# Four-layer cross-attention kernel: the joint last stage with its context in four groups of 32 rows, and the narrow layer's scores made twice instead of its probabilities being turned

## Chip, cores and metric

One core of one Trainium2 chip. The metric is the device time of one execution in microseconds (us), median over the runs. Everything is fp32.

## What is computed

`x` is [32 batches, 128 tokens, 128], the context is [32, 128, 96]. Four layers follow each other; all have 16 heads:

```python
x = L0(x, ctx)   # self-attention + cross-attention, heads 64 wide, then a gated feed-forward
x = L1(x, ctx)   # cross-attention, heads 8 wide, layer norm, feed-forward, residual
# L2, wide (heads 64 wide):
h = layernorm(x, gamma, beta)
Q, K, V = h @ Wq, ctx @ Wk, ctx @ Wv              # 128 -> 1024, 96 -> 1024, 96 -> 1024
x = x + (softmax(Q K^T) * 64**-0.5) V @ Wo + bo
# L3, narrow (heads 8 wide), no layer norm:
q, k, v = x @ Wq^T, ctx @ Wk^T, ctx @ Wv^T        # 128 -> 128, 96 -> 128, 96 -> 128
x = x + softmax(q k^T * 8**-0.5) v @ Wo^T + bo
```

## The kernel before, in words

Every stage is a block of five hand-written instruction streams (PE, ACT, DVE, POOL, SP) that meet through semaphores. `wide_attention` does L0's two attentions, `feed_forward` L0's feed-forward, `text_attention` L1's attention, `feed_forward` L1's, and `wide_and_narrow` does L2 and L3 together. That last one is the joint last stage, and almost all of the change lies in it.

The stage is a software pipeline over steps `t`. In each step every batch-level operation is done once, for a batch `t + lag`. `step` in each engine's stream writes out the order; the steps 4 to 27 are a hardware loop of four steps a turn (`steps`), the others are written out. The wide layer runs ahead (queries and keys of batch t+2, scores of t+1, weighing of t-1), the narrow layer behind (h and keys of t-1, scores of t-2, the rest of t-3).

PSUM has eight banks. Four are `scores`: the wide scores of a batch fill all four (two in slot 0, two in slot 1), and later in the step the narrow scores of another batch fill the same four. The other four are the ring: `order` (L1290 on) lists twenty fills a step, each fill takes the next bank, and PE may start one when the fill four places before it has been emptied by ACT or DVE.

What the wide layer does, per batch: `w_queries` and `w_keys` (PE, `project_T`, L1484) make the transposed queries and keys in two halves of 4 matmuls each, with 96 context rows for the keys; POOL copies the context of the batch to `w_cT` first. `w_score` (L1450) is 16 matmuls on two row tiles of 64. DVE takes the maxima of both slots and subtracts them in slot 1; ACT exponentiates slot 0 head by head with its sums (`w_exponentiate_0`, 4 heads twice) and slot 1 in one go. POOL divides (`w_divide`), DVE turns 32x32 squares, and SP sends them to DRAM and back (`away`, `back`) so that they land transposed; `w_weigh` (L1529) multiplies them with the values, `w_project_out` (L1569) is 8 matmuls, `w_finish` adds the residual. `w_values` (L1509) is two matmuls of 512 columns over 96 rows.

What the narrow layer does, per batch: POOL copies the rows of x and the context; `n_queries_keys` makes both in one bank; POOL sets the keys of four heads apart with a mask (`n_set_keys_apart`), so that `n_score` (L1467) makes all 16 heads in 4 matmuls of 512 columns on four row tiles of 32, one per bank. DVE and ACT make the softmax as in the wide layer. `n_transpose_probs` (L1477) turns all 16 heads on PE, 16 transposes in four ring banks, which ACT copies back; `n_weigh` (L1542) weighs them, the inverse sums are turned too (L1550), and `n_weighed` multiplies.

`text_attention` (L1's attention) already works in another way, which the change takes over for L3: scores are made once with queries on the partitions (`scores_for_max`, L1017) only so that DVE can find the maxima (L1195), PE turns the maxima, DVE appends them to the queries' spare rows, and the scores are made a second time, already less their maximum and with the keys on the partitions (`scores_less_max`, L1029). Their exponentials need no transposing before they are weighed (L1061). There the maxima banks and the score banks are three each.

## Time and profile before

| | us |
|---|---|
| runs of the kernel before | 1679.09, 1668.0, 1674.45 |
| median | 1674.45 |
| the profiled execution | 1676.32 |
| its span, first to last instruction | 1674.6 |
| mean granted TensorE clock of it | 0.99 |
| joint last stage, from its first matmuls to the end of the span | 1099.6 to 1674.6 |

The profile is of one execution. Busy time of PE is of overlapping matmuls, so what one group of matmuls costs is read from the start of its first to the start of the group behind it, not from its duration. A fp32 matmul is two records ("x8" is four matmuls), a fp32 transpose is one.

### The profile page before, as it was taken

Reading aid. Unit: us, or ns where it says so; the run is one execution under the profiler, and the core shown is the slowest. Engines: PE = TensorE matmul, PEld = TensorE weight load, DVE = VectorE, ACT = ScalarE, POOL = GpSimd, SP = SyncE. Lnnn points to the kernel's source line nnn. Section 1 sums busy time; section 2 is a strip of 40 time slices with the busy share of each in tenths; the row PEclk is TensorE's granted clock in tenths of the full one; section 3 lists DMA queues with packets and bytes.
Section 4 is the critical chain, followed back from the end, with each engine's and each line's share of the span. In section 5 each row is a group of like instructions: output and inputs, shape, how many; then the busy total and the mean of one; then the engine's idle time right before and its main releaser. Section 6 shows DMA issues by size and latency. Waiting matters only on the chain. (4 is left out here: it accounts for less than half of the span.)

```text
span 1674.6 us, 48052 instructions
## 1 busy us (share of the span) xinstructions
PE 1620.9 (97%) x16480; PEld 1348.4 (81%) x16480; DVE 1252.0 (75%) x2424; ACT 1174.7 (70%) x3648; POOL 704.6 (42%) x1027
## 2 busy tenths in 40 slices
PE   7999999999999999989999998988999999999998
PEld 5788888888888888879978887876888888888876
DVE  4877777777777777757767775656888888888885
ACT  4777777777777777743336665455888888888886
POOL 3444444454444444332224442643343444444441
PEclk9999999999999999999999999998999999999999
DMA  6777777788667776740000000014343444344440
GB/s 185 202 190 189 185 189 191 201 217 218 186 183 199 184 186 182 202 135 1 0 2 3 3 3 2 0 40 138 120 142 119 141 120 139 121 139 121 139 130 9
DMA packets 225246, 211.60 MB, mean 126 GB/s; under 512 B 19475, under 2 KB 222805, under 8 KB 225109
## 3 DMA queue, kind: packets, MB, share of 16 engines
q1 hardware_dynamic: 225108, 209.92, 45.4%
q8 instruction: 67, 1.10, 0.3%
q14 instruction: 71, 0.57, 0.1%
HBM read 109.72 MB, written 100.14 MB: 125 GB/s over the span
## 5 line engine op out<-in xcount | busy, mean ns | idle before, releaser
L907 POOL TENSOR_TENSOR L_probs<-L_probs,L_inv_sum 128x1024 f32<-128x1024 f32 x128 | 242.8, 1897 | 87.2 <-DVE L_inv_sum L803 87.2
L691 ACT ACTIVATE L_probs<-L_scores,L_neg_max 128x128 f32<-128x128 f32 x512 | 182.8, 386 | 135.0 <-DVE L_neg_max L783 135.0
L777 DVE TENSOR_REDUCE L_row_max<-L_scores 128x8 f32<-128x1024 f32 x128 | 156.2, 1220 | 41.8 <-PE L_scores L549 41.8
L2128 POOL TENSOR_TENSOR L2L_w_probs<-L2L_w_probs,L2L_w_inv_sum 128x1024 f32<-128x1024 f32 x64 | 121.4, 1896 | 124.2 <-DVE L2L_w_inv_sum L1931 123.7
L809 DVE STREAM_TRANSPOSE L_squares<-L_probs 128x1024 f32<-128x1024 f32 x125 | 153.0, 1224 | 0.3 <-POOL L_probs L907 0.3
L549 PE MATMUL L_scores<-L_kT,L_qT 64*128 64x128 f32 x2048 | 131.8, 278 | 0.9 <-ACT L_kT L680 0.9
L600 PE MATMUL L_ring<-L_probsT,L_v 128*64 128x128 f32 x2048 | 126.6, 276 | 3.9 <-issue 1.8
L600 PEld LDWEIGHTS L_ring<-L_probsT,L_v 128*64 128x64 f32 x2048 | 110.5, 137 | 23.9 <-issue 19.6
L549 PEld LDWEIGHTS L_scores<-L_kT,L_qT 64*128 64x128 f32 x2048 | 119.4, 188 | 12.5 <-ACT L_oT L680 8.1
L793 DVE TENSOR_REDUCE L_sums<-L_probs 128x8 f32<-128x1024 f32 x64 | 78.1, 1220 | 64.8 <-ACT L_probs L698 64.8
L1195 DVE TENSOR_REDUCE L_maxima<-L_s_banks 128x4 f32<-128x512 f32 x128 | 87.5, 688 | 44.6 <-PE L_s_banks L1017 44.6
L1695 ACT ACTIVATE L2L_w_probs<-L2L_scores,L2L_w_neg_max 128x128 f32<-128x128 f32 x256 | 90.4, 371 | 41.7 <-DVE L2L_w_neg_max L1895 41.7
L691 ACT ACTIVATION_READ_ACCUMULATOR L_probs<-L_scores,L_neg_max 128x1 f32 x512 | 115.8, 226 | 0.0
L680 ACT ACTIVATE L_oT<-L_ring 128x512 f32<-128x512 f32 x128 | 76.5, 599 | 39.7 <-PE L_ring L600 39.6
L1884 DVE TENSOR_REDUCE L2L_w_row_max<-L2L_scores 128x8 f32<-128x1024 f32 x64 | 76.7, 1198 | 28.8 <-PE L2L_scores L1450 28.8
L1706 ACT ACTIVATE L2L_n_probs<-L2L_scores,L2L_n_neg_max 128x128 f32<-128x128 f32 x256 | 90.7, 377 | 4.8 <-DVE L2L_n_neg_max L1901 4.1
L1253 POOL TENSOR_SCALAR L_k_apart<-L_qk,quad_mask 128x128 f32<-128x128 f32 x116 | 50.3, 448 | 93.2 <-ACT L_qk L1153 93.2
L680 ACT ACTIVATE L_kT<-L_ring 128x512 f32<-128x512 f32 x128 | 76.8, 600 | 18.2 <-PE L_ring L557 18.2
L2104 POOL TENSOR_TENSOR L2L_n_x_bias<-L2L_n_rows_h,bias_L 128x128 f32<-128x128 f32 x32 | 14.6, 456 | 177.9 <-DVE x L1980 177.8
L680 ACT ACTIVATE L_qT<-L_ring 128x512 f32<-128x512 f32 x128 | 76.2, 595 | 17.3 <-PE L_ring L557 12.0
L1126 ACT ACTIVATE L_exps<-L_t_banks 128x512 f32<-128x512 f32 x128 | 69.4, 597 | 19.7 <-PE L_t_banks L1029 19.7
L1684 ACT ACTIVATE L2L_n_probsT<-L2L_ring 128x512 f32<-128x512 f32 x128 | 70.4, 611 | 17.9 <-PE L2L_ring L1477 17.9
(236 smaller groups left out, 4578.7 us busy)
## 6 DMA issues: line engine op xcount, KB each, us to landing
L_relay<-L_squares SPq DMA_DIRECT2D x125, 512.0 KB, 3.4
L_probsT<-L_relay SPq DMA_DIRECT2D x500, 128.0 KB, 3.7
L2L_relay<-L2L_w_squares SPq DMA_DIRECT2D x62, 512.0 KB, 3.4
L2L_w_probsT<-L2L_relay SPq DMA_DIRECT2D x248, 128.0 KB, 2.9
out_x<-x SPq DMA_DIRECT2D x32, 64.0 KB, 2.7
L0a_wq<-in_L_xattn_Wq SPq DMA_DIRECT2D x2, 256.0 KB, 2.9
L0a_wk<-in_L_xattn_Wk SPq DMA_DIRECT2D x2, 256.0 KB, 3.2
L0a_wv<-in_L_xattn_Wv SPq DMA_DIRECT2D x1, 512.0 KB, 6.3
```

Source lines behind the costliest of these rows:

```text
L549: last = nc.tensor.matmul(scores[:, s, r, i, :], q[part, i, at.n % 2, :], k[part, i, at.n % 2, :], start=True, stop=True, tile_position=(h ...
L600: last = nc.tensor.matmul(to[WIDE * r:WIDE * (r + 1), TOKENS * i:TOKENS * (i + 1)], v[:, at.n % 2, WIDE * h:WIDE * (h + 1)], probsT[:, at. ...
L680: nc.scalar.activation(to, src, ACT.Copy).then_inc(emptied["act"], 1)
L691: done = nc.scalar.activation(slot_probs(at, 0)[:, n, :], scores[:, 0, r, i, :], ACT.Exp, scale=layer_of(at).scale, bias=neg_max[:, n:n + ...
L777: nc.vector.tensor_reduce(row_max[:, s, :], slot(s), AX.X, ALU.max).then_inc(max_ready[s], 1)
L793: nc.vector.tensor_reduce(sums[:, :, 1, :], slot_probs(at, 1).rearrange("p (r i) k -> p r i k", r=2), AX.X, ALU.add).then_inc(sum_ready, 1)
L809: nc.vector.transpose(squares[:, at.n % 2, :, SLOT_HEADS * s:SLOT_HEADS * (s + 1), :] .rearrange("p j h a -> p h j a"), slot_probs(at, s). ...
L907: nc.gpsimd.tensor_tensor(to, to, inv_sum[:, :, s, :].unsqueeze(3) .to_broadcast([TOKENS, 2, GROUP, TOKENS]), ALU.mult).then_inc(divided, 1)
L1195: nc.vector.tensor_reduce(maxima[:, b % 2, g, :, 0:1].rearrange("p j d -> p (j d)"), s_bank(b, g), AX.X, ALU.max, negate=True).then_inc(ma ...
L1695: done = nc.scalar.activation(w_slot(at, 0)[:, h, :], scores[:, 0, r, i, :], ACT.Exp, scale=W.scale, bias=w_neg_max[:, h:h + 1], accum_out ...
L1706: done = nc.scalar.activation(n_slot(at, 0)[:, h, :], scores[:, 0, r, i, :], ACT.Exp, scale=N.scale, bias=n_neg_max[:, h:h + 1], accum_out ...
L2128: nc.gpsimd.tensor_tensor(to, to, w_inv_sum[:, :, s, :].unsqueeze(3) .to_broadcast([TOKENS, 2, GROUP, TOKENS]), ALU.mult).then_inc(w_divid ...
```

## The change

The stage keeps its place and its results; what changes:

- **Context.** A new class `ContextBlocks` holds the transposed context cut into three blocks of 32 rows, each of them four times: on partitions 0-31, 32-63, 64-95 and 96-127. During `text_attention` SP writes `ctxT` to DRAM once and loads eight batches at a time back into one of two buffers, 12 DMAs each; the chunks for batches 16 to 31 are loaded in the stage, at steps 8 and 16. `w_cT` and `n_cT` with POOL's copies go.
- **Keys and values.** The weights are stored per group g of four: `L2_wk` [128, 3, 2, 128], `L2_wv` [128, 3, 256], loaded by 24 DMAs instead of two. `w_keys` is 24 matmuls of 128 columns (three accumulated per result) and `w_values` 12 of 256 columns, each group on its own row tile of 32 and in its own ring bank. Values are now made at step t for batch t.
- **Scores.** `w_score` is cut in two halves with the keys of the next batch between them.
- **Narrow layer.** As in `text_attention`: `n_score_for_max`, `n_find_maxima`, `n_transpose_maxima`, `n_append_maxima`, `n_score_less_max`, `n_exponentiate`, `n_weigh`, then `n_turn_back`, `n_divide`, `n_transpose_o`, `n_project_out`. The 16 transposes of probabilities, the turned inverses, the row sums and POOL's copy of x go. The maxima use slot 0 and the second scores slot 1, two banks each.
- **Who does what.** POOL normalises x for L2 (was DVE), ACT scales the turned h (was DVE).
- **Written out.** All 40 steps are written out; there is no loop and no special last step. The last wide batch's probabilities are turned by PE at the head of step 32.

```diff
-    order = [("w.PV0", -1, "act"), ("w.PV1", -1, "act"), ("w.q0", 2, "act"), ("w.k0", 2, "act"),
-             ("n.T0", -3, "act"), ("n.T1", -3, "act"), ("w.Wo", -1, "dve"), ("n.T2", -3, "act"), ("n.T3", -3, "act"),
...
+    order = [*((f"w.k{g}", 2, "act") for g in CHUNKS_4), ("n.mT", -3, "dve"), ("w.PV0", -1, "act"),
+             ("w.PV1", -1, "act"), ("n.PV", -4, "act"), ("w.q0", 2, "act"), ("n.D", -4, "dve"), ("w.Wo", -1, "dve"),
+             *((f"w.v{g}", 0, "act") for g in CHUNKS_4), ("n.hT", -1, "act"), ("n.oT", -4, "act"),
+             ("w.q1", 2, "act"), ("n.qk", -1, "act"), ("n.v", -3, "act"), ("n.Wo", -4, "dve"), ("w.hT", 3, "act")]
...
+            def n_score_for_max(b, g, h):
+                part = slice(QUAD * g, QUAD * (g + 1))
+                if h == 0:
+                    if g == 0:
+                        pe.wait_ge(n_parts_ready, b + 1)
+                    if g >= 2:
+                        pe.wait_ge(n_max_ready, 4 * b + g - 1)
+                    elif real(b + 3):
+                        pe.wait_ge(w_exp_ready[0], 2 * (b + 3) + 2)
...
+                last = nc.tensor.matmul(s_bank(g)[:, 2 * (1 - h):2 * (1 - h) + 2, :],
+                                        n_q_part[part, b % 2, h, :], n_k_apart[part, b % 2, 2 * h:2 * h + 2, :],
+                                        start=True, stop=True, tile_position=(QUAD * g, 0))
...
+            def w_keys(b):
+                ctx_blocks.await_loaded(pe, b)
+                to = [start_fill(f"w.k{g}", b) for g in CHUNKS_4]
+                for c in range(2):
+                    for r in range(3):
+                        for g in CHUNKS_4:
+                            part = slice(QUAD * g, QUAD * (g + 1))
+                            last = nc.tensor.matmul(to[g][:, TOKENS * c:TOKENS * (c + 1)], W.wk[part, r, c, :],
+                                                    ctx_blocks.of(b)[part, r, :], start=r == 0, stop=r == 2,
+                                                    tile_position=(QUAD * g, 0))
...
+            for t in range(first, last + 1):
...
+                if real(t - 2):
+                    n_find_maxima(t - 2, 0)
+                    n_find_maxima(t - 2, 1)
+                if real(t + 1):
+                    w_add_up(t + 1)
+                if real(t - 2):
+                    n_find_maxima(t - 2, 2)
+                    n_find_maxima(t - 2, 3)
...
+                if t >= 1 and t % ContextBlocks.CHUNK == 0 and t // ContextBlocks.CHUNK + 1 < ContextBlocks.COUNT:
+                    await_filled(sp, "w.v3", t - 1)
+                    ctx_blocks.load(sp, t // ContextBlocks.CHUNK + 1)
```

How the order moves, on PE, from the head of a step. In the first piece L1450 is the wide scores, L1529 the weighing, L1484 queries and then keys, L1477 the turned narrow probabilities, L1569 the output projection, L1467 the narrow scores, L1550 the turned inverses, L1561 the turned x. This is before:

```order
L1450 MATMUL L2L_scores<-L2L_w_kT,L2L_w_qT 128x128 x16
L1529 MATMUL L2L_ring<-L2L_w_probsT,L2L_w_v 64x128 x16
L1484 MATMUL L2L_ring<-L2L_w_hT,L_wq 128x128 x4
L1484 MATMUL L2L_ring<-L2L_w_cT,L_wk 128x128 x4
L1477 MATMUL L2L_ring<-ident,L2L_n_probs 128x128 x8
L1569 MATMUL L2L_ring<-L_wo,L2L_w_oT 128x128 x8
L1467 MATMUL L2L_scores<-L2L_n_k_apart,L2L_n_qT 128x512 x4
L1477 MATMUL L2L_ring<-ident,L2L_n_probs 128x128 x8
L1550 MATMUL L2L_ring<-ident,L2L_n_inv_wide 128x128
L1484 MATMUL L2L_ring<-L2L_w_hT,L_wq 128x128 x4
L1561 MATMUL L2L_ring<-ident,L2L_n_rows_h 128x128
L1484 MATMUL L2L_ring<-L2L_w_cT,L_wk 128x128 x4
```

And now, PE from the head of a step to the output projection (lines of the changed kernel: L1445 wide scores, L1509 keys, L1567 the turned maxima, L1536 weighing, L1579 narrow weighing, L1497 queries, L1590 the weighed rows turned back, L1556 output projection):

```order
L1445 MATMUL L2L_scores<-L2L_w_kT,L2L_w_qT 128x128 x8
L1509 MATMUL L2L_ring<-ctx_blocks,L_wk 128x128 x24
L1445 MATMUL L2L_scores<-L2L_w_kT,L2L_w_qT 128x128 x8
L1567 MATMUL L2L_ring<-ident,L2L_n_maxima 128x128
L1536 MATMUL L2L_ring<-L2L_w_probsT,L2L_w_v 64x128 x16
L1579 MATMUL L2L_ring<-L2L_n_exps,L2L_n_v 32x128 x16
L1497 MATMUL L2L_ring<-L2L_w_hT,L_wq 128x128 x4
L1590 MATMUL L2L_ring<-ident,L2L_n_weighed 128x128 x2
L1556 MATMUL L2L_ring<-L_wo,L2L_w_oT 128x128 x8
```

The keys moved between the halves of the scores, the transposes of probabilities are gone, and the narrow weighing moved ahead of the first queries. Behind it the two narrow score calls, with the values between them, and the end of the step (the second pair of L1460 and L1476 rows of each call reads like the first and is left out here):

```order
L1460 MATMUL L2L_scores<-L2L_n_k_apart,L2L_n_q_part 128x256 x2
L1476 MATMUL L2L_scores<-L2L_n_q_part,L2L_n_k_apart 128x128 x4
...
L1520 MATMUL L2L_ring<-L_wv,ctx_blocks 128x256 x12
L1460 MATMUL L2L_scores<-L2L_n_k_apart,L2L_n_q_part 128x256 x2
L1476 MATMUL L2L_scores<-L2L_n_q_part,L2L_n_k_apart 128x128 x4
...
L1596 MATMUL L2L_ring<-ident,x 128x128
L1600 MATMUL L2L_ring<-ident,L2L_n_rows_o 128x128
L1497 MATMUL L2L_ring<-L2L_w_hT,L_wq 128x128 x4
L1606 MATMUL L2L_ring<-L2L_n_hT,L_wqT 128x128
L1607 MATMUL L2L_ring<-ctxT,L_wkT 128x128
```

The values, which ended the step, now stand between the two calls. On SP's queue at step 8, in the changed kernel (L2000 stores a batch, L2036 loads context, L1984 and L1993 take squares to DRAM and back):

```order
L2000 DMA out_x<-x 128x128
L2036 DMA ctx_blocks<-ctx_turned 32x1024 x12
L1984 DMA L2L_relay<-L2L_w_squares 512x1x256
L1993 DMA L2L_w_probsT<-L2L_relay 32x4x256 x4
L1984 DMA L2L_relay<-L2L_w_squares 512x1x256
L1993 DMA L2L_w_probsT<-L2L_relay 32x4x256 x4
```

The twelve loads are issued ahead of the step's relays; the other steps have the same rows without them.

## Rows read from the trace of the kernel before

**Rows 1.** Busy time in three stretches of the last stage: start, even steps, end (PE, PEld, DVE, ACT, POOL; then PEclk, DMA share, GB/s).
```profile
1099.58:1183.06 83.48, 71.68 (x630) 57.46 (x630) 54.31 (x98) 52.19 (x174) 30.03 (x44) 0.92 0.33 102
1183.06:1617.76 434.70, 432.09 (x4761) 363.62 (x4762) 375.07 (x645) 380.62 (x1327) 183.71 (x258) 1.00 0.44 131
1617.76:1674.60 56.84, 45.77 (x506) 35.96 (x504) 33.73 (x58) 40.77 (x139) 13.44 (x18) 0.94 0.13 40
```
**Rows 2.** PE's timeline in one even step: start us, us, line, out<-in, records.
```profile
1300.19 2.06 PE L1450 MATMUL L2L_scores<-L2L_w_kT,L2L_w_qT 64*128 64x128 f32 x32
...
1305.07 1.06 PE L1484 MATMUL L2L_ring<-L2L_w_cT,L_wk 96*128 96x128 f32 x8
1305.96 1.04 PE L1477 MATMUL L2L_ring<-ident,L2L_n_probs 128*128 128x128 f32 x8
1306.84 1.95 PE L1569 MATMUL L2L_ring<-L_wo,L2L_w_oT 128*128 128x128 f32 x16
1308.72 1.14 PE L1467 MATMUL L2L_scores<-L2L_n_k_apart,L2L_n_qT 32*128 32x512 f32 x8
1309.79 1.09 PE L1477 MATMUL L2L_ring<-ident,L2L_n_probs 128*128 128x128 f32 x8
...
1311.83 1.06 PE L1484 MATMUL L2L_ring<-L2L_w_cT,L_wk 96*128 96x128 f32 x8
1312.82 1.08 PE L1542 MATMUL L2L_ring<-L2L_n_probsT,L2L_n_v 128*32 128x128 f32 x32
...
1314.60 1.02 PE L1509 MATMUL L2L_ring<-L_wv,L2L_w_cT 96*128 96x512 f32 x2
1315.46 0.39 PE L1575 MATMUL L2L_ring<-L_woT,L2L_n_oT 128*128 128x128 f32 x2
...
1316.86 2.06 PE L1450 MATMUL L2L_scores<-L2L_w_kT,L2L_w_qT 64*128 64x128 f32 x32
```
**Rows 3.** PE's timeline in L1's attention: one call of both scores and what follows.
```profile
922.27 0.48 PE L1017 MATMUL L_s_banks<-L_k_apart,L_q_part 32*128 32x256 f32 x2
922.28 0.49 PE L1029 MATMUL L_t_banks<-L_q_part,L_k_apart 32*128 32x128 f32 x4
922.59 0.38 PE L1017 MATMUL L_s_banks<-L_k_apart,L_q_part 32*128 32x256 f32 x2
...
922.81 0.38 PE L1017 MATMUL L_s_banks<-L_k_apart,L_q_part 32*128 32x256 f32 x2
...
923.38 0.33 PE L1050 MATMUL L_b_bank<-ident,L_maxima 128*128 128x128 f32 x1
923.63 1.08 PE L1061 MATMUL L_a_bank<-L_exps,L_v 128*32 128x128 f32 x32
```
**Rows 4.** The page's costliest groups, whole span: busy us, mean ns, idle before and releaser.
```profile
L2128 POOL TENSOR_TENSOR L2L_w_probs<-L2L_w_probs,L2L_w_inv_sum 128x1024 f32<-128x1024 f32 x64 | 121.4, 1896 | 124.2 <-DVE L2L_w_inv_sum L1931 123.7
L1195 DVE TENSOR_REDUCE L_maxima<-L_s_banks 128x4 f32<-128x512 f32 x128 | 87.5, 688 | 44.6 <-PE L_s_banks L1017 44.6
L1695 ACT ACTIVATE L2L_w_probs<-L2L_scores,L2L_w_neg_max 128x128 f32<-128x128 f32 x256 | 90.4, 371 | 41.7 <-DVE L2L_w_neg_max L1895 41.7
L1884 DVE TENSOR_REDUCE L2L_w_row_max<-L2L_scores 128x8 f32<-128x1024 f32 x64 | 76.7, 1198 | 28.8 <-PE L2L_scores L1450 28.8
L1253 POOL TENSOR_SCALAR L_k_apart<-L_qk,quad_mask 128x128 f32<-128x128 f32 x116 | 50.3, 448 | 93.2 <-ACT L_qk L1153 93.2
L1126 ACT ACTIVATE L_exps<-L_t_banks 128x512 f32<-128x512 f32 x128 | 69.4, 597 | 19.7 <-PE L_t_banks L1029 19.7
```
**Rows 5.** Groups by line, 690 to 960 us and 1180 to 1670 us: two kinds of weight load.
```profile
L1029 PEld LDWEIGHTS L_t_banks<-L_q_part,L_k_apart 32*128 32x128 f32 x624 | 37.9, 186 | 0.0
...
L1484 PEld LDWEIGHTS L2L_ring<-L2L_w_hT,L_wq 128*128 128x128 f32 x416 | 50.4, 191 | 4.5 <-issue 4.5
```
**Rows 6.** SP's timeline at the end of L0's attention, one weight load; and DMA issues, the relay.
```profile
732.84 0.43 SPq L187 DMA_DIRECT2D L_wk<-in_L_xattn_Wk  x1
...
L2L_relay<-L2L_w_squares SPq DMA_DIRECT2D x62, 512.0 KB, 3.4
```

More of the change, by code:

```diff
@@ L1296, in wide_and_narrow @@
     LANDED = 16 * SQUARES
-    ring = Ring(order, range(first, last + 1), BATCHES,
-                {LAST_WIDE: last_wide_order, **tail_orders})
+    ring = Ring(order, range(first, last + 1), BATCHES, {LAST_WIDE + 1: turned_by_pe + order})
     chunks = INNER // 128
@@ L1471, in n_transpose_probs @@
-            def n_transpose_probs(at, n):
-                s, r = divmod(n, 2)
-                if r == 0:
-                    pe.wait_ge(n_exp_ready[s], at.times(2, 2) if s == 0 else at.times(1, 1))
-                to = start_fill(f"n.T{n}", at)
-                for i in range(GROUP):
-                    last = nc.tensor.transpose(to[:, TOKENS * i:TOKENS * (i + 1)],
-                                               n_slot(at, s)[:, GROUP * r + i, :], ident[:, :])
-                filled_by(last, f"n.T{n}")
@@ new lines, in w_values @@
+            def w_values(b):
+                to = [start_fill(f"w.v{g}", b) for g in CHUNKS_4]
+                for r in range(3):
+                    for g in CHUNKS_4:
+                        part = slice(QUAD * g, QUAD * (g + 1))
+                        last = nc.tensor.matmul(to[g][:, 0:INNER // 4], ctx_blocks.of(b)[part, r, :], W.wv[part, r, :],
+                                                start=r == 0, stop=r == 2, tile_position=(QUAD * g, 0))
+                        if r == 2:
+                            filled_by(last, f"w.v{g}")
@@ new lines, in n_turn_back, with n_transpose_h @@
+            def n_turn_back(b):
+                await_emptied(pe, "n.PV", b)
+                to = start_fill("n.D", b)
+                for half in range(2):
+                    last = nc.tensor.transpose(to[:, TOKENS * half:TOKENS * (half + 1)], n_weighed[:, half, :],
+                                               ident[:, :])
+                filled_by(last, "n.D")
+            def n_transpose_h(b):
+                await_emptied(pe, "w.Wo", b)
+                filled_by(nc.tensor.transpose(start_fill("n.hT", b)[:, 0:TOKENS], x[:, b, :], ident[:, :]), "n.hT")
@@ new lines, in _, with __init__, of, write @@
+                if real(t + 1) and t + 1 != LAST_WIDE:
+                    away(t + 1, 0)
+                    back(t + 1, 0)
+            sp.wait_ge(stored, 16 * BATCHES)
+class ContextBlocks:
+    CHUNK = 8
+    COUNT = BATCHES // CHUNK
+    ROWS = 32
+    def __init__(self, tile, dram, written, loaded):
+        self.tile, self.dram, self.written, self.loaded = tile, dram, written, loaded
+    def of(self, b):
+        return self.tile[:, b // self.CHUNK % 2, :, b % self.CHUNK, :]
+    def write(self, sp, ctxT):
+        sp.dma_start(self.dram, ctxT[0:CTX, :, :]).then_inc(self.written, 16)
+        sp.wait_ge(self.written, 16)
+    def load(self, sp, n):
+        src = self.dram.rearrange("(r p) b t -> p r b t", p=self.ROWS)
+        for g in range(4):
+            for r in range(CTX // self.ROWS):
+                sp.dma_start(self.tile[self.ROWS * g:self.ROWS * (g + 1), n % 2, r, :, :],
+                             src[:, r, self.CHUNK * n:self.CHUNK * (n + 1), :]).then_inc(self.loaded[n % 2], 16)
+    def await_loaded(self, engine, b):
+        n = b // self.CHUNK
+        engine.wait_ge(self.loaded[n % 2], 16 * 12 * (n // 2 + 1))
```

1140 lines of the change are left out of this document (466 added, 674 removed).

## The prediction

> **What bounds the kernel now.** I read the page's slices first: PE is busy at nine tenths or more nearly everywhere, at the full clock. Then the windows of the stage that changes. In its even middle, 26 steps take 434.70 us, that is 16.72 us a step, and PE is busy 432.09 of it [rows 1]; the other engines have room (ACT 380.62 / 26 = 14.6 us a step, DVE 14.4, POOL 7.1). The reader should see that there nearly nothing waits: PE's timeline of one step runs from 1300.19 to 1316.86, 16.67 us, with each group starting where the one before ends [rows 2]. So a step is the sum of what PE is given, and an instruction taken off PE is worth its whole slot until another engine becomes the bound. At the stage's start (83.5 us, clock 0.92) and end (56.8 us) it is different: PE is busy 71.68 and 45.77 us, and chains of waits decide [rows 1].
>
> **PE's work in a step, part by part.** Slots are from the start of one group to the start of the next.
>
> Removed: two groups of eight transposes, 1306.84 - 1305.96 = 0.88 us for the first and about 0.93 for the second, and the turned inverses, one transpose, 0.88 / 8 = 0.11 [rows 2]. Together -1.92.
>
> Narrow scores: the one call of 1.07 us (1308.72 to 1309.79 [rows 2]) becomes two calls of the kind that L1's attention has, each 923.38 - 922.27 = 1.11 us [rows 3]. +1.15. The turned maxima cost 923.63 - 923.38 = 0.25 there. Three more transposes (two turned back, one of the divided rows) are 0.33. Together +1.73.
>
> Keys: 0.89 (1305.07 to 1305.96) and 0.99 (1311.83 to 1312.82), 1.88 in all [rows 2]. The trace has no row for 24 matmuls on four row tiles. In L1's call the four tiles together finish one round, 128 columns of two passes on each, every 0.22 us (922.59 to 922.81), and 0.32 for the first round (922.27 to 922.59), behind a change of tiling [rows 3]. 24 matmuls are six such rounds: 0.32 + 5 x 0.22 = 1.42. -0.46. The lower end would be that, the upper end is worked out below. Values: 0.86 twice (1314.60 to 1315.46), 1.72 [rows 2]; now 12 matmuls of 256 columns, three a tile, again six rounds, behind a group of the same tiling: 1.31. -0.41.
>
> Changes of tiling: each costs some 0.1 at the first round (0.32 against 0.22 [rows 3]). The scores are cut in two by the keys, which adds two such changes beyond those counted, and narrow weighing now stands behind wide weighing, which is no dearer. +0.2.
>
> Sum: 16.68 - 1.92 + 1.73 - 0.46 - 0.41 + 0.2 = 15.8 us of PE a step. The queries, wide scores, wide weighing (16 matmuls), output projection and narrow weighing stay.
>
> Here a page's rule speaks against the keys. The rows show a weight load of 32x128 at 186 ns and one of 128x128 at 191 ns [rows 5], so cutting 96 rows in three makes three loads of full length out of one. The Trainium skill, TensorE: Matmul & The Clock Gate, section LDWEIGHTS, says just that: the time goes by the columns, not by the rows. If loads went one behind the other it would undo the gain. But L1's call shows 24 of them (12 matmuls of two) in 1.11 us, 46 ns apiece, so loads of different row tiles overlap; the Trainium skill, TensorEngine Tiling (Array Packing), Key Properties, agrees that tiles load and multiply independently. What no row shows is a round with eight of these loads instead of six. Bound from the row: if six loads were just what fits in 0.22 us, eight take 0.29, and the keys cost 6 x 0.07 = 0.44 us more. I take nothing of it, since L1's narrow weighing runs 32 loads, if narrow ones, in 1.08 us, and keep 0.44 for the range.
>
> **Waits in the new step.** I laid one step out from the durations. Start of wide scores 0; second half done at 3.4 (1.0 + 1.42 + 1.0). DVE: second row maxima and subtraction, 1.2 each [rows 4], then the appended maxima, two 128x128 operations, 0.6 by my estimate from 0.69 for 512 columns [rows 4]: 6.7. The ring bank of the first queries is the one of the turned maxima, so the queries start at 6.8; PE alone would be there at 6.7. Queries full at 7.9; ACT copies (0.5) and does four heads of the wide exponentials (4 x 0.37, overlapping by a tenth: 1.4 [rows 4]): 9.9. The first narrow call waits for them, because it uses the same banks; PE would be there at 9.9 too. That call to 11.0; then the values cover DVE's two maxima (2 x 0.69 [rows 4]) and ACT's two exponentials (2 x 0.60 [rows 4]): second call at 12.4, where PE alone would have started at 12.3. To 13.5, then 0.3 + 0.9 + 0.5 + 0.5, and the last fill of the ring waits for ACT's copy of the second queries until about 15.8. Step 16.0. So I take 0.2 us of waits on top of 15.8. Queued behind the waiting narrow call are values, second queries and the next step's scores, and behind these all of DVE's and ACT's next step; there is no cover for a longer wait.
>
> Room elsewhere: DVE loses two row maxima, the subtraction and the sums of the narrow layer (4 x 1.2) and gets four maxima (2.8) and small ones, so about 13 of 16. ACT loses four copies of a bank and the eight heads with accumulators and gets four exponentials: 11 to 12. POOL gets six operations of 0.45 [rows 4] beside two divisions of 1.9 [rows 4] and the normalising: 8.5. Its longest order, division, then the six, is done at about 7.5, ahead of the narrow call at 9.9. None of the three bounds by its sum.
>
> 26 steps x (16.72 - 16.0) = -18.7 us.
>
> **Start, end, transfers.** Start: the narrow layer's x no longer goes through POOL's queue, and values are a step later. Laid out the same way, the first three steps come to 10 to 14 us less than before; but part of what was lost there is a clock of 0.92 with PE busy 71.68 of 83.48 us [rows 1], which a less busy PE won't better. I take -7, between 0 and -14. End: one wide weighing and projection moves a step later and the two narrow calls have no values between them (1.3 us of waits twice), while the last full steps are shorter: +1, between -5 and +8.
>
> SP: a DMA occupies its queue 0.43 us [rows 6]. The 24 loads instead of two at the end of L0's attention are 22 x 0.47 = 10 us, which there ends beside PE's tail with about as much room; +0.5, between 0 and 3. During L1's attention SP has nothing else. In the stage, 12 context loads (5.6 us of queue, 1.57 MB) stand twice ahead of a relay that is due at about 8 us of the step. It goes off about 4 us late and behind those bytes; it needs 3.4 us out [rows 6], and about 5 us for its four parts to be issued and to land; it has about 5 us of room. +4 for both, between 0 and 12. Written-out code instead of a loop: L1's attention is written out as well and keeps 0.22 us rounds [rows 3]; 0.
>
> Sum: -18.7 - 7 + 1 + 0.5 + 4 = -20.2 us. The profiled execution took 1676.3 (span 1674.6 and 1.7 around it), so 1656.1 on its terms; the median shown is 1.9 below the profiled one, well inside the 11 us that the three runs spread over. I forecast 1656.
>
> **Rivals.**
>
> *PE alone decides* (0.2). The three tight places do not wait and the start gives all of its 14: 26 x 0.2 = 5 and 7 more off: 1644. For it: the step before shows no waits with ACT at 14.6 of 16.7. Against: the banks of the maxima are two here and three in L1.
>
> *Weight loads bind the keys* (0.12). 26 to 31 batches x 0.44 = 11 to 14 more: 1668. For it: 186 ns a load whatever the rows [rows 5]; against: 24 of them in 1.11 us.
>
> *The context loads delay the relay* (0.1). 12 instead of 4: 1664, two steps longer by 6 us each and nothing else.
>
> *Handovers, slower than before* (0.13). The chain wide scores - DVE - queries - ACT - narrow call - DVE - second call - end of step has about eight handovers between engines, and I gave each 0.1 to 0.2 us. My chain is as long as PE's own work, so every bit more lands on the step: it is even with before at 0.09 us more each (0.72 / 8), and at 0.2 more the step is 17.6, 26 x 0.9 = +23: 1676 + 23 - 1.5 = 1698. In L1's attention DVE's maxima already waited 44.6 us in all for scores [rows 4], a sign that the loop of scores and maxima is a loop of latencies; there three banks hid it. Against: most of these places have cover of another group on PE.
>
> *It doesn't do what it says.* If rows of 32 did not run side by side, keys would take 24 x 0.22 = 5.3 us. L1's call excludes it.
>
> The forecast itself has 0.45.
>
> **How the numbers follow.** The forecast's own range is 1648 to 1665. For 8 in 10: the low end takes PE alone, with some of the end, 1638; the high end takes loads binding and a few tenths of handovers, 1676; beyond lie 0.08 above and about as much below. A measurement of this kernel tells about 1% from no change, 16.7 us, so faster means under 1657.7: all of PE alone, and seven tenths of the forecast's weight, some of the small rivals: 0.56. Same, up to 1691: 0.34. Slower: 0.10, the far part of the handovers.
>
> **What would show it.** Right: even steps of 15.9 to 16.2 us in PE's timeline; keys 1.4 us and values 1.3 from their start to the next group; no idle before the second narrow call above 0.2; ACT about 12 us a step. Wrong: rounds of the keys at 0.29 us; PE idle before L1460 on ACT's exponentials or DVE's maxima by more than 0.3; idle before L1536 at steps 9 and 17 of over 3 us; a step over 16.6.

## The result, and the profile after

The changed kernel takes 1689.3 us (median of 6 runs, 1683.2 to 1693.4), the kernel before 1674.4 (6 runs): a ratio of 1.0087, 95% interval 1.0057 to 1.0117. The forecast was 1656, with 1638 to 1676 as the range. What was measured lies 13 us above the range, in what the prediction had as "Same, up to 1691" (chance 0.34). It was wrong, in size and in sign.

The two profiled spans are 1688.1 and 1674.6 us, 13.5 apart. Four stretches hold all of it. The windows of the last stage after, in the columns of [rows 1]:

```profile
core 0: us, PE busy (x) PEld busy (x) DVE busy (x) ACT busy (x) POOL busy (x), PEclk, DMA share, GB/s
1108.66:1182.55 73.89, 63.61 (x894) 56.72 (x894) 47.51 (x83) 47.43 (x160) 36.24 (x52) 0.95 0.38 115
1182.55:1620.75 438.20, 426.13 (x6812) 386.42 (x6811) 310.82 (x566) 315.41 (x1016) 226.38 (x334) 1.00 0.46 138
1620.75:1688.10 67.35, 55.56 (x717) 46.16 (x716) 25.30 (x57) 28.76 (x81) 18.73 (x33) 0.83 0.13 40
```

| stretch | before [rows 1] | after | difference | forecast |
|---|---|---|---|---|
| ahead of the last stage | 1099.58 | 1108.66 | +9.1 | +0.5 |
| its start | 83.48 | 73.89 | -9.6 | -7 |
| 26 even steps | 434.70 | 438.20 | +3.5 | -18.7 |
| its end | 56.84 | 67.35 | +10.5 | +1 |

So there are three causes to find, and one of them lies 350 us ahead of the last stage. (For the context loads, which fall into the even steps, the forecast had +4 besides.) The even step is 16.85 us (438.20 / 26), not 16.0. PE's timeline of one of them:

```profile
start us, us, engine line op out<-in xcount [idle before <-releaser]
1317.27 1.16 PE L1445 MATMUL L2L_scores<-L2L_w_kT,L2L_w_qT 64*128 64x128 f32 x16
1318.37 1.62 PE L1509 MATMUL L2L_ring<-ctx_blocks,L_wk 32*128 32x128 f32 x48
1319.92 1.16 PE L1445 MATMUL L2L_scores<-L2L_w_kT,L2L_w_qT 64*128 64x128 f32 x16
1321.01 0.33 PE L1567 MATMUL L2L_ring<-ident,L2L_n_maxima 128*128 128x128 f32 x1
...
1327.58 0.48 PE L1460 MATMUL L2L_scores<-L2L_n_k_apart,L2L_n_q_part 32*128 32x256 f32 x2 [0.17 <-ACT L2L_w_probs L1681]
...
1329.97 0.57 PE L1460 MATMUL L2L_scores<-L2L_n_k_apart,L2L_n_q_part 32*128 32x256 f32 x2
...
1331.36 0.33 PE L1596 MATMUL L2L_ring<-ident,x 128*128 128x128 f32 x1
...
1333.20 0.39 PE L1617 MATMUL L2L_ring<-L_woT,L2L_n_oT 128*128 128x128 f32 x2
1333.79 0.30 PE L1562 MATMUL L2L_ring<-ident,L2L_w_rows_h 128*128 128x128 f32 x1 [0.20 <-ACT L2L_w_qT L1670]
1334.13 0.38 PE L1445 MATMUL L2L_scores<-L2L_w_kT,L2L_w_qT 64*128 64x128 f32 x2
```

Read as in [rows 2], from one start to the next: keys 1.55 us, the two narrow calls with the values between them 3.78 (1327.58 to 1331.36), and two places where PE waits for ACT. They look small, 0.17 and 0.20, but the second leaves 0.59 between the starts of the two last fills for work of 0.22.

The 26 steps are not all alike. Steps 4 to 28 take 16.83 to 16.88 us and step 29, the last of the stretch, 16.22; but step 17, right behind the second context load, takes 17.89, and there PE stands still between the two halves of the weighing. SP's issues of step 16, then PE in step 17:

```profile
1390.64 5.43 SPq L2036 DMA_DIRECT2D ctx_blocks<-ctx_turned  x12
1396.16 0.52 SPq L1984 DMA_DIRECT2D L2L_relay<-L2L_w_squares  x1
1402.10 1.75 SPq L1993 DMA_DIRECT2D L2L_w_probsT<-L2L_relay  x4
```

```profile
1407.45 1.09 PE L1536 MATMUL L2L_ring<-L2L_w_probsT,L2L_w_v 128*64 128x128 f32 x16 [0.89 <-ACT L2L_w_oT L1670]
```

The profile names ACT's copy, which was done at 1407.29, but by the trace the last of the relay's four parts landed at 1407.36, and PE's next matmul starts 0.09 us later. The way out to DRAM behind the context loads took 5.9 us (1396.16 to 1402.10) where the page's median is 3.2. So the context loads cost about 1.05 us here, and the other steps take 16.83.

Ahead of the stage, the end of L0's attention and the start of L0's feed-forward. SP's issues there first (the last of the 24 pieces), then PE, after:

```profile
743.13 0.57 SPq L188 DMA_DIRECT2D L_wk<-in_L_xattn_Wk  x1
743.74 0.58 SPq L188 DMA_DIRECT2D L_wv<-in_L_xattn_Wv  x1
...
749.77 0.58 SPq L188 DMA_DIRECT2D bias_L<-in_L_xattn_bo  x1
```

```profile
744.56 2.05 PE L644 MATMUL L_ring<-L0b_wo,L_oT 128*128 128x128 f32 x16
750.81 4.60 PE L131 MATMUL L0ff_gate<-ident 128*128 128x128 f32 x20 [4.20 <-PEq L404]
...
758.12 1.06 PE L2136 MATMUL L0ff_gate<-L0ff_hT,wp 128*128 128x256 f32 x2
...
763.24 0.70 PE L2136 MATMUL L0ff_gate<-L0ff_hT,wp 128*128 128x256 f32 x2
```

The same place before:

```profile
743.74 2.05 PE L625 MATMUL L_ring<-L0b_wo,L_oT 128*128 128x128 f32 x16
746.45 2.47 PE L131 MATMUL L0ff_gate<-ident 128*128 128x128 f32 x20 [0.66 <-PEq L385]
...
751.70 0.60 PE L2284 MATMUL L0ff_gate<-L0ff_hT,wp 128*128 128x256 f32 x2
```

An issue takes 0.57 us and not the 0.43 of [rows 6]. SP ends at 750.35, PE's last group at 746.61, and the block ends with the later of them: PE is idle 4.20 us for 0.66. Then its granted clock is at the lower level, 0.50 of full speed from 750.81 to 763.24: the twenty records of `keep_clock` take 4.60 us for 2.47, and until 763.24 the feed-forward's groups stand 0.85 apart for 0.43. The sum: PE 0.82 late already, 3.54 of wait, 2.13, and six groups times 0.42, 2.5: 9.0 of the 9.1 us. Each of these is one execution against one; the medians of experiment 1 put the loads at 6.2 us.

### The profile page after: what moved, and what is told of

It is laid out like the page before. It is cut to its first block and busy times, and to the rows that moved or that the text cites. A ratio compares the mean times of both kernels' runs of the same rounds, so it can differ in the third digit from the quotient of the medians.

```text
span 1688.1 us, 51406 instructions
## 1 busy us (share of the span) xinstructions
PE 1622.8 (96%) x19008; PEld 1386.1 (82%) x19008; DVE 1172.6 (69%) x2330; ACT 1094.0 (65%) x3264; POOL 760.0 (45%) x1126
## 5 line engine op out<-in xcount | busy, mean ns | idle before, releaser
L1841 DVE TENSOR_REDUCE L2L_n_maxima<-L2L_scores 128x4 f32<-128x512 f32 x128 | 82.4, 687 | 32.0 <-PE L2L_scores L1460 32.0
L1691 ACT ACTIVATE L2L_n_exps<-L2L_scores 128x512 f32<-128x512 f32 x128 | 69.7, 602 | 27.4 <-PE L2L_scores L1476 27.4
L1670 ACT ACTIVATE L2L_w_kT<-L2L_ring 128x256 f32<-128x256 f32 x128 | 38.8, 389 | 71.6 <-PE L2L_ring L1509 71.6
L1460 PE MATMUL L2L_scores<-L2L_n_k_apart,L2L_n_q_part 32*128 32x256 f32 x512 | 77.4, 396 | 7.5 <-ACT L2L_w_probs L1681 5.1
```

What stands on the lines that cost most here:

```text
L1460: last = nc.tensor.matmul(s_bank(g)[:, 2 * (1 - h):2 * (1 - h) + 2, :], n_q_part[part, b % 2, h, :], n_k_apart[part, b % 2, 2 * h:2 * h + ...
L1691: nc.scalar.activation(n_exps[:, b % 2, GROUP * g:GROUP * (g + 1), :].rearrange("p h q -> p (h q)"), t_bank(g).rearrange("p j q -> p (j q) ...
```

## Experiments

All ratios are to the kernel before (1674 to 1675 us), with the 95% interval. The heads of the even steps and the windows are read as above. Apart from experiment 4, whose interval reaches past it, all of these kernels lie less than 2% from the kernel before, so differences are small and are told with their intervals. A profile is of one execution, which need not be the median one.

### 1. The loads, somewhere else

The whole list of L2's loads moves from the last step of L0's attention to `first_context_blocks`, which SP runs in L1's attention.

```diff
-            if t == 2 * BATCHES:
-                load_norm(sp, "L2", "L2_ln", "L2_xattn_gamma", "L2_xattn_beta")
...
             ctx_blocks.load(sp, 1)
+            load_norm(sp, "L2", "L2_ln", "L2_xattn_gamma", "L2_xattn_beta")
+            load(sp, "L2", W["L2", "q"][:, :], a["L2_xattn_Wq"])
...
```

> The changed kernel with all loads of the last stage's wide layer issued by SP in L1's attention, behind the first two context blocks, instead of the last step of L0's attention. Theory (SP's 24 issues of 0.58 us end after TensorE's last matmul there, the block's end waits for them, and TensorE's clock is low for some 12 us after): L0ff's first matmuls start about 4.3 us earlier than in the changed kernel, at about 746.5, at the higher clock, L0ff's own turn near 758.6, and the last stage's first matmuls near 1100; time about 1680 (1677 to 1683), which still is above the kernel before, since the last stage alone is 4.4 us longer. Rival (the pieces are hidden, and the 9 us before the last stage come from elsewhere, such as the placement of the tiles): time within 2 us of 1689.

Measured: 1683.1 us, 1.0053 (1.0037 to 1.0068), at the upper end of what was expected. The idle time at the block's end is 0.66 again, and the last stage begins at 1096.93. So the loads' place is the cause of what was lost ahead of the stage. The time fell by 6.2 us and not by 9: in this execution the stage's start took 77.94 us at a clock of 0.91 instead of 73.89 at 0.95. Step 16.85, end 68.3, as after. Whether that start is chance or comes of the move stayed open; in the eight kernels below that are built on this one, the last stage begins anywhere from 1096.2 to 1102.1 and its start takes 73.7 to 78.4 us, so a single profile can't tell a difference of 5 or 6 us there from chance.

### 2. The pieces alone, in the kernel before

```diff
-                load_wide(sp, "L2", "L2", "", CTX)
...
+                for g in range(4):
+                    for r in range(CTX // 32):
+                        for w in ("k", "v"):
+                            load(sp, "L2", W["L2", w][32 * r:32 * (r + 1), 256 * g:256 * (g + 1)],
+                                 a[f"L2_xattn_W{w}"][32 * r:32 * (r + 1), 256 * g:256 * (g + 1)])
...
```

> The kernel before, where alone the last stage's key and value weights are loaded in 24 pieces of 32 rows and 256 columns, with nothing else changed. Theory: SP's issues end some 5 to 10 us later, behind TensorE's end of L0's attention, so time 1674.4 plus 7 to 10, about 1683, all of the loss ahead of the last stage (its start near 1108), the stage itself 575 us. Rival (cost hidden beside TensorE's tail, as the prediction had it): +0.5 us, at most 3.

Measured: 1675.5 us, 1.0008 (0.9991 to 1.0025). No loss that can be measured. The theory as I had put it fell, and the timeline says why. SP, then PE:

```profile
744.42 0.42 SPq L187 DMA_DIRECT2D L_wv<-in_L_xattn_Wv  x1
744.88 0.43 SPq L187 DMA_DIRECT2D L_wo<-in_L_xattn_Wo  x1
745.36 0.58 SPq L187 DMA_DIRECT2D bias_L<-in_L_xattn_bo  x1
```

```profile
746.39 2.47 PE L131 MATMUL L0ff_gate<-ident 128*128 128x128 f32 x20 [1.25 <-PEq L392]
```

As many transfers with as many bytes, but 0.42 us each, not 0.57. SP ends at 745.94, beside PE's tail to within a microsecond, and behind that wait of 1.25 us the granted clock is still 1.00. The number of pieces was not the cost; their form is what differs.

### 3. Which form

```diff
                 for g in range(4):
                     for r in range(CTX // 32):
                         load(sp, "L2", W["L2", "k"][32 * g:32 * (g + 1), r, :, :], keys[g][:, r, :, :])
+                for g in range(4):
+                    for r in range(CTX // 32):
                         load(sp, "L2", W["L2", "v"][32 * g:32 * (g + 1), r, :], values[g][:, r, :])
```

> The changed kernel with its 24 pieces still issued at the end of L0's attention, but all 12 of the keys (three-dimensional: two runs of 128 columns) ahead of all 12 of the values (one run of 256 columns). Theory (an issue of 0.58 us is due to the form of the keys' pieces, and the values' pieces took as long only because they stood behind one): keys 0.57 us, values 0.42 to 0.45 as in before_pieces; SP ends at 748.5 instead of 750.4, TensorE waits about 2.4 us instead of 4.2 at the block's end; if that wait still lowers the clock, time 1687, if it does not, 1683. Rival (both forms take 0.58 here whatever their order): time 1689.

Measured: 1684.4 us, 1.0061 (1.0040 to 1.0082).

```profile
734.60 8.22 SPq L188 DMA_DIRECT2D L_wk<-in_L_xattn_Wk  x12
742.86 5.69 SPq L188 DMA_DIRECT2D L_wv<-in_L_xattn_Wv  x12
```

```profile
750.10 4.04 PE L131 MATMUL L0ff_gate<-ident 128*128 128x128 f32 x20 [2.23 <-PEq L406]
...
756.94 0.59 PE L2143 MATMUL L0ff_value<-L0ff_hT,wp 128*128 128x256 f32 x2
```

From start to start a keys' piece (32 rows of two runs of 128 columns) takes 0.69 us and a values' piece (32 rows of one run of 256) 0.47, that is 0.43 and the gap. The two together are 0.58 in the mean: in the changed kernel the dear and the cheap ones shared it. The Trainium skill, DMA: Bandwidth & Descriptors, section "Why a DMA increments its semaphore by 16 and not by 1", says that "One descriptor moves one contiguous run of the last dim", so a keys' piece needs twice as many; and the Trainium skill, Perfetto Trace Analysis, DMA Instruction — HWDGE, counts the wait for the descriptor generator into the time shown for an issue, which would be why a values' piece looks dear behind a keys' piece. That these are the mechanism no run here shows. Behind PE's wait of 2.23 us the clock was still low, but only until the feed-forward's groups (0.59 us at 756.94, where 0.59 is the higher level). SP ended only 0.7 us earlier than after (749.64) and PE's last group 1.3 later. The profiled spans are 2.4 us apart, all of it ahead of the last stage (1106.32); the medians are 4.9 apart. The theory had the cause right and the keys' price too low (0.57 expected), so SP ended 1.1 us later than it said.

### 4. Without the row tiles

The keys and values in their old form, from `ctxT`; the narrow layer and the written-out code as changed. The context blocks and their loads are gone, ScalarE copies two banks of 512 columns where it copied four of 256, and the values, the ring's order and the weights' loads change to match (not shown).

```diff
             def w_keys(b):
-                ctx_blocks.await_loaded(pe, b)
-                to = [start_fill(f"w.k{g}", b) for g in CHUNKS_4]
-                for c in range(2):
-                    for r in range(3):
-                        for g in CHUNKS_4:
...
+                for n in range(2):
+                    to = start_fill(f"w.k{n}", b)
+                    for c in range(4):
+                        last = nc.tensor.matmul(to[:, TOKENS * c:TOKENS * (c + 1)],
+                                                W.wk[0:CTX, BANK * n + 128 * c:BANK * n + 128 * (c + 1)],
+                                                ctxT[0:CTX, b, :], start=True, stop=True)
+                    filled_by(last, f"w.k{n}")
```

> The changed kernel with the key and value projections in their old form (96 rows of ctxT, 8 matmuls of 128 columns and 2 of 512, two fills each, no context blocks, weights loaded in two transfers as before): only the new narrow layer and the written-out code are left of the change. If the row tiles bring what the prediction took (-0.87 us a step), the even step is 17.5 to 17.7 against 16.84 of the changed kernel; if they bring only what their slots show (keys 1.55 for 1.88, values inside the narrow scores), 17.2 to 17.4; if the fewer and wider copies of ScalarE and the missing change of tiling give it back, 16.8. Ahead of the last stage no delay (start near 1099.6), so time about 1674.4 + 5 + 10 + 26 x (step - 16.72) less 9 for the start: 1690 to 1705 by the first, 1682 to 1690 by the second.

Measured: 1706.2 us, 1.0187 (1.0154 to 1.0220). The step:

```profile
1317.59 1.16 PE L1432 MATMUL L2L_scores<-L2L_w_kT,L2L_w_qT 64*128 64x128 f32 x16
1318.68 2.05 PE L1493 MATMUL L2L_ring<-ctxT,L_wk 96*128 96x128 f32 x16
1320.66 1.16 PE L1432 MATMUL L2L_scores<-L2L_w_kT,L2L_w_qT 64*128 64x128 f32 x16
...
1328.33 0.48 PE L1447 MATMUL L2L_scores<-L2L_n_k_apart,L2L_n_q_part 32*128 32x256 f32 x2 [0.17 <-ACT L2L_w_probs L1660]
...
1332.65 0.33 PE L1575 MATMUL L2L_ring<-ident,x 128*128 128x128 f32 x1
...
1335.31 0.38 PE L1432 MATMUL L2L_scores<-L2L_w_kT,L2L_w_qT 64*128 64x128 f32 x2
```

17.72 us, just above what the first branch expected. The row tiles, with the copies that go with them, bring 17.72 - 16.85 = 0.87 us a step, which is what the forecast had: 0.43 at the keys (1.98 to 1.55) and 0.54 at the values between the narrow calls (4.32 to 3.78), less 0.1 for the way from the last fill back to the wide scores. PE waits for ACT at the same two places and for as long in both kernels, so no wait has moved. Steps 9 and 17 are as long as the others here, 17.71, which ties the 1.05 us of step 17 to the context loads. The rival of weight loads that bind the keys (0.44 us a step) is excluded at that price: they take 0.13 more than forecast, and no run tells whether loads are a part of it. And the rest of the change, forecast at +0.2 us a step, costs 17.72 - 16.72 = +1.0. The error is there.

### 5. The handovers on ScalarE

```diff
+                if real(t + 1):
+                    w_exponentiate_0(t + 1, 1)
                 if real(t + 2):
                     w_queries(t + 2, 0)
                 if real(t + 1):
-                    w_exponentiate_0(t + 1, 1)
                     w_exponentiate_1(t + 1)
...
                     n_exponentiate(t - 3, 0)
-                    n_exponentiate(t - 3, 1)
                 if real(t + 2):
                     w_queries(t + 2, 1)
+                if real(t - 3):
+                    n_exponentiate(t - 3, 1)
```

> late_loads with two moves on ScalarE in the last stage alone: the second four exponentials of the wide layer ahead of the copy of the first queries, and the copy of the second queries between the last two exponentials of the narrow layer. TensorE's program is the same. Theory (about 0.5 us of an even step are two handovers, TensorE's narrow scores 0.17 us late behind ScalarE's exponentials and the last fill 0.36 us late behind the copy of the second queries): even step 16.35 to 16.5 against 16.85, time 8 to 12 us below late_loads (1671 to 1675). Rival (TensorE's records already fill the step, or the copy that moves makes another fill wait): step 16.8 to 16.9, time 1683.

> late_loads with only the second of act_order's two moves: ScalarE copies the second queries between the last two narrow exponentials. act_order's step was 16.40 us against 16.85. If the last fill's wait (0.2 us and the gap of 0.15 ahead of it) is the larger part, the step is 16.5 to 16.55 and the time 1674 to 1676; if the wait of the narrow scores for the exponentials (0.17 us) is nearly all, 16.7 and 1679; if the copy that comes late in its turn is a cost, above 16.85.

Measured: both moves 1670.0 us, 0.9967 (0.9947 to 0.9986); the second alone 1677.1, 1.0013 (0.9997 to 1.0028). With both:

```profile
1195.60:1606.14 410.54, 406.48 (x6549) 370.90 (x6549) 298.77 (x544) 300.08 (x976) 217.65 (x321) 1.00 0.48 142
```

25 steps of 16.42 us in the mean, PE idle for 4 us in 410. The mean holds two long steps: behind the context loads, step 9 takes 17.40 us and step 17 18.05, in all 2.8 us more than their neighbours, where the changed kernel lost 1.05. The shorter step leaves the delayed relay 0.5 us less room, and at step 8 the relay itself took longer (10.5 us from its first issue to its last landing, for 9.4). The other steps take 16.31, against 16.83. PE's program is untouched, and so is the sum of what ACT does; with the second move alone the step is 16.52, as its text had for the larger part. So two places where ACT copied or exponentiated in the wrong order cost 0.52 us a step, 11 us in all when the longer steps 9 and 17 are counted, although the profile's waits gave PE only 5.0 and 4.5 us in all there (the changed kernel, in 25 and 26 steps):

```profile
PE L2L_ring L1562 <- ACT L2L_w_qT L1670: 5.0, 25, 0.2
PE L2L_scores L1460 <- ACT L2L_w_probs L1681: 4.5, 26, 0.2
```

From start to start, the output projection and the wait behind it take 1.89 us for 2.12, and the last two fills stand 0.27 apart for 0.59. With both moves:

```profile
1302.71 1.95 PE L1555 MATMUL L2L_ring<-L_wo,L2L_w_oT 128*128 128x128 f32 x16
1304.60 0.48 PE L1459 MATMUL L2L_scores<-L2L_n_k_apart,L2L_n_q_part 32*128 32x256 f32 x2
...
1310.32 0.39 PE L1616 MATMUL L2L_ring<-L_woT,L2L_n_oT 128*128 128x128 f32 x2
1310.59 0.30 PE L1561 MATMUL L2L_ring<-ident,L2L_w_rows_h 128*128 128x128 f32 x1
```

### 6. The wide scores in one piece

```diff
                     w_score(t + 1, 0)
+                    w_score(t + 1, 1)
                 if real(t + 2):
                     w_keys(t + 2)
-                if real(t + 1):
-                    w_score(t + 1, 1)
```

> late_loads with both halves of the wide scores one behind the other and the keys behind them, so that TensorE goes from row tiles of 64 to row tiles of 32 once and not back. Theory (the split costs 0.19 us and the way back from the keys 0.1): even step 16.55 to 16.7 against 16.85, 4 to 7 us less than late_loads, and scores in one group of 2.0 us. Rival (the keys between the halves hide a wait for the narrow exponentials or for ScalarE's last copies, which now shows at the second half): step 16.85 or more.

> Both edits at once. If their gains are of different causes they add: even step 16.1 to 16.3, time 1665 to 1671, below the kernel before (1674.4). If the second only moves a wait that the first removed, the step is that of the better one alone.

Measured: 1690.5 us, 1.0090 (1.0060 to 1.0120), step 17.20; with act_order's moves 1680.2, 1.0037 (1.0017 to 1.0057), step 16.67.

```profile
1315.87 2.06 PE L1444 MATMUL L2L_scores<-L2L_w_kT,L2L_w_qT 64*128 64x128 f32 x32
1317.86 1.62 PE L1508 MATMUL L2L_ring<-ctx_blocks,L_wk 32*128 32x128 f32 x48
1320.02 0.30 PE L1566 MATMUL L2L_ring<-ident,L2L_n_maxima 128*128 128x128 f32 x1 [0.55 <-ACT L2L_w_kT L1668]
```

The scores in one piece take 1.99 us for 2.19, as expected; but the turned maxima go to the ring bank of the first keys, and now wait 0.55 us for ACT's copy of it. The split costs 0.2 and covers 0.55. My theory priced the work and overlooked the cover; the rival, which named another place, had the sign. With act_order's moves neither expectation held (16.1 to 16.3, or the better edit's step alone): the edit costs 0.37 us a step in one kernel and 0.36 in the other, so the two effects are independent and add.

### 7. The end

First, fillers wherever a step waits, 84 of them from step 33 on:

```diff
+            def kept(to, t):
+                if t > LAST_WIDE + 1:
+                    keep_clock(nc, to[:, 0:TOKENS], ident, 6)
+                return to
```

> As late_loads, and in the steps from 33 on TensorE runs six 128x128 multiplications of the identity into the bank that it is about to fill, before it waits for that fill's operand (they change no result). Theory (the end is long by low clock and by chains of handovers, about 3 us by the clock): granted clock of the last 68 us above 0.95 instead of 0.83, and 2 to 4 us less than late_loads. Rival (the chain of handovers alone sets the end, or the fillers are in its way): within 1 us of late_loads, or up to 3 us more.

Measured: 1690.3 us, 1.0099 (1.0063 to 1.0136), 7 us more than without. The clock of the end rose to 0.96, and its length to 76.9 us. The fillers are some 18 us of PE at the higher clock, and stood in the way. That tells nothing on the clock's price, so the next try put 19 of them only where PE waits (the expectation below says 25; PE has 38 more records, two to a matmul), and another kernel changed the order instead, on PE as here in steps 34 and 32, with ScalarE's stream and the ring likewise:

```diff
+                if t == LAST_WIDE + 3:
+                    n_transpose_maxima(t - 3)
+                    n_values(t - 3)
+                    n_weigh(t - 4)
+                    n_both_scores(t, (0, 1), (2, 3))
+                    n_turn_back(t - 4)
+                    n_both_scores(t, (2, 3), (0, 1))
+                    n_transpose_o(t - 4)
+                    n_project_out(t - 4)
...
                 n_both_scores(t, (0, 1), (2, 3))
+                if t == LAST_WIDE + 1:
+                    n_transpose_h(t - 1)
+                    n_queries_keys(t - 1)
```

> act_order with another order of its last steps on TensorE and ScalarE: in step 32 the last batch's turn to columns and its narrow queries and keys stand between the two halves of the narrow scores (behind them before), and in step 34 the last batch's scores stand on both sides of the turn back of batch 30, with its values ahead (all behind that turn before). Theory (the end is 11 us longer than before because each step of the narrow layer there is one chain of handovers of about 10 us): the stretch from the head of step 30 to the end, 67.96 us in act_order, becomes 61 to 65, time 1665 to 1668. Rival (low clock sets it, and shorter waits of the same number leave it): 67 to 68 us, time 1670.

> act_order with 25 multiplications of the identity (0.22 us each at the higher clock) put by TensorE where it waits from step 33 on: four ahead of the last batch's first narrow scores, two or three at five other waits, two ahead of the last turn to columns. They change no result. Theory (low clock from about step 33 makes TensorE's work there 4 to 5 us longer, for instance the 32 matmuls of the narrow weighing 1.93 us for 1.08): granted clock of the last 68 us above 0.93 for 0.81, and that stretch 63 to 66 us, time 1666 to 1669. Rival (the fillers take as much as they give, as the 84 of tail_clock did): 67 to 69 us.

> tail_order and tail_fill in one kernel (act_order, late_loads and the changed kernel under it). If chain and clock are two causes, the last stretch is 58 to 61 us, near the 56.8 of the kernel before, and the time 1661 to 1665, faster than the kernel before by 0.6 to 0.8 %. If either contains the other, it is that of the better one.

Measured: order 1667.4 us, 0.9954 (0.9939 to 0.9968); fillers 1667.8, 0.9952 (0.9936 to 0.9969); both 1664.6, 0.9943 (0.9923 to 0.9963). The last has two fillers more, 21. The windows from the head of step 30 to the end, of act_order, tail_order, tail_fill and tail_both, one each:

```profile
1606.14:1674.10 67.96, 56.40 (x717) 47.12 (x716) 25.30 (x57) 28.93 (x81) 18.73 (x33) 0.81 0.14 39
```

```profile
1603.87:1667.90 64.03, 53.08 (x717) 43.95 (x716) 25.27 (x57) 29.14 (x81) 18.70 (x33) 0.87 0.14 42
```

```profile
1606.83:1670.00 63.17, 55.10 (x755) 46.81 (x754) 25.27 (x57) 28.93 (x81) 18.70 (x33) 0.97 0.14 42
```

```profile
1599.59:1661.30 61.71, 53.00 (x759) 45.32 (x758) 25.25 (x57) 29.02 (x81) 18.64 (x33) 0.99 0.14 43
```

In these executions order alone gives 3.9 us back, clock alone 4.8, both 6.3, so the last stretch is 61.7 us where 58 to 61 was expected. By the medians it is 2.6, 2.2 and 5.4 us against act_order's 1670.0. The end also differs between executions: it takes 65.5 to 68.3 us at a clock of 0.80 to 0.86 in the eight kernels whose end was not touched, and each of the three new ones lies below that. So chain and clock are both causes. That they share a part, since the new order alone also raises the clock from 0.81 to 0.87, fits the windows, but the medians add up, and it isn't shown. One group shows the clock, the narrow weighing of the last batch, in act_order and in tail_both:

```profile
1666.34 1.93 PE L1578 MATMUL L2L_ring<-L2L_n_exps,L2L_n_v 128*32 128x128 f32 x32 [0.40 <-ACT L2L_n_exps L1690]
```

```profile
1655.15 1.08 PE L1596 MATMUL L2L_ring<-L2L_n_exps,L2L_n_v 128*32 128x128 f32 x32
```

Some 5 of the 10.5 us remain, and 3.2 us at steps 9 and 17 (17.98 and 17.86 us for 16.31) behind the context loads, which no experiment touched alone. The kernel before had orders of its own for the last five steps, with the last wide batch weighed a step earlier and a narrow layer a step shorter; taking that back was not tried.

tail_both is the fastest of all: 10 us under the kernel before and 25 under the change as it was made, with the same work in every even step. The 10 us are 0.6% of the time.

## Why the prediction was wrong, point by point

- *Row tiles.* Right: -0.87 us a step forecast, 0.87 measured by undoing them; keys 1.55 for 1.42, the values' part better than thought. The keys' 48 loads of 32x128 lie within 1.55 us, 32 ns apiece against 186 for one alone [rows 5], so loads of different row tiles do overlap. Of the rules of the Trainium skill that were weighed, the trace agrees with both: with TensorE: Matmul & The Clock Gate, LDWEIGHTS, on one load (186 and 191 ns [rows 5]), and with TensorEngine Tiling (Array Packing), Key Properties, on loads of different tiles.
- *PE's sum of 15.8 us.* This step failed first. It is too low by 0.5: with the two waits gone the step is 16.31 (experiment 5). Keys +0.13; the narrow calls with the values 3.78 for 3.53, +0.25 (the sum took the call of [rows 3], which stands between other groups; that this is the reason isn't shown); the last two fills and the way back to row tiles of 64, about +0.2, for which the sum had nothing; other groups are 0.1 cheaper. The sum starts from a step of 16.68 and the gain from the mean of 16.72; in the trace before, every fourth step (one turn of the loop) takes 16.89 and the others 16.67, and written out no step does that. The 0.2 for the split scores was right (2.19 for 1.99).
- *"I take 0.2 us of waits on top."* 0.52 (16.83 less 16.31). From the head of the step the layout had the first narrow call at 9.9, the second at 12.4 and the last fill at 15.8; they start at 10.31, 12.70 and 16.52 (1327.58, 1329.97 and 1333.79 less 1317.27). The layout made ACT's chain and PE's own work tie at the narrow call ("PE would be there at 9.9 too"), and a tie between two sums worked out is not a zero. The rival of slower handovers was this mechanism, at a price of 0.3 instead of 1.6 us a step over the forecast's; its 1698 was too far. It had a chance of 0.13, though the prediction left only 0.08 above 1676.
- *Start, -7.* -9.6, inside its bounds. In part that is luck: the same stretch took 73.1 to 78.4 us in the other kernels, which is -10.4 to -5.1.
- *End, +1, between -5 and +8.* +10.5, outside. It counted the waits of the two calls, not that each narrow step at the end is one chain of some 10 us, nor that waits of 0.3 to 1.1 us in a row would bring the clock down: from 1664.6 on it is 0.50, and over the whole end 0.83 for 0.94.
- *The 24 loads, +0.5, between 0 and 3.* +9.1 ahead of the stage in the profile, 6.2 by the medians of experiment 1; outside either way. The place was seen and the room was judged; the duration failed. 0.43 us from [rows 6] is that of a plain matrix, and the keys' pieces take 0.69. With 0.42 the cost is what was forecast (experiment 2). And the bound knew only the time that SP is late, not what a low clock makes of it: 3.5 us of wait became 8.2 (3.54, 2.13 and 2.5).
- *Context loads, +4.* +1.05, inside its bounds: nothing at step 9, and at step 17 a wait of 0.89 us, not before the weighing but between its halves. The room for the late relay was judged a little too small, and it shrinks with the step: 2.8 us in act_order, 3.2 in tail_both.

Sum of the misses: 8.6 ahead of the stage, 21.2 in the even steps, 9.5 at the end, less 2.6 and 3.0 for the start and the context loads: 33.7, from 1656.1 to the 1689.8 of the profiled execution. So nearly two thirds of the miss are the even step, 0.5 us of work on PE and 0.3 us of waits that the layout by hand did not have.

## What to carry to other kernels

When a change cuts one transfer into many, price an issue by a row of the same form (rows times runs), and ask what its queue is the last to finish: here a block's end that waited 4 us cost the clock as well. Where the trace shows an engine nearly full and its waits as small, try the order on the engine that hands over to it before anything else: two moves on ScalarE were worth more than half of what the row tiles brought (0.52 and 0.87 us a step). Look at every step by itself before taking a mean: the mean of 16.85 hid one step that waited a microsecond for a transfer. A new order for the even steps needs one of its own for the last ones.

## What the chip showed that was not expected

- An issue on SP took 0.42 us for 32 rows of one run of 1 KB, 0.69 from start to start for 32 rows of two runs of 512 bytes, and 0.43 for a whole matrix of 96 rows [rows 6].
- TensorE's clock behind an idle time at a block's end: after 0.66 and 1.25 us of it the next twenty records took 2.47 us, the higher level; after 2.23 us 4.04, and after 4.20 us 4.60 and another 8 us of groups at the lower one. The work ahead of it is the same in all four, but each is one execution, and in the one with 2.23 us the clock had also been low once shortly before (0.51 from 730.20 to 733.60).
- Two waits that the profile puts at 0.37 us a step together gave back 0.52: from start to start the two places shrank by 0.23 and 0.32, since the gap ahead of the wait went with it (at the last fill 0.59 from start to start for work of 0.22, where the profile shows a wait of 0.20).
- A releaser that the profile names can be the wrong one of two: at step 17 it names ACT's copy, done at 1407.29, while the transfer that landed at 1407.36 was the last thing the matmul needed.
